# VectorE takes over the subtractions that split projected node rows, with four places for a group's rows

## The chip, the cores and the metric

The kernel runs on one core of a Trainium2 chip. The metric is the device time of one execution in microseconds (us); lower is better. Engines: TensorE (PE, and PEld for its weight loads), VectorE (DVE), ScalarE (ACT), GpSimd (POOL) and SyncE (SP), whose instructions here only issue DMAs.

## The reference

A graph attention layer and a mixture-of-experts layer, over 6250 nodes of 256 values and 100000 edges sorted by target:

```python
h = (layernorm(x) @ W.T).reshape(n, H, D)                 # H = 8 heads, D = 32
enc = relu(edge_attr @ edge_W.T + edge_b).reshape(-1, H, D)
alpha = einsum(h[src], a_src) + einsum(h[dst], a_dst) + sum(enc * h[dst], -1)
alpha = where(alpha >= 0, alpha, 0.2 * alpha)
ex = exp(alpha - segment_max(alpha, dst)[dst])
attn = ex / maximum(segment_sum(ex, dst)[dst], 1e-10)
x = x + (segment_sum(h[src] * attn[..., None], dst).reshape(n, H * D) + bias)
# then: x = x + top-2-of-8 experts (layernorm(x)), each gelu(xe @ W1 + b1) @ W2 + b2
```

The change is in the part that makes `h` and the tables of it.

## The kernel before

The program is five stages, one after the other, each its own block with a barrier of all engines at its end: `prepare`, `edges`, `attend`, `route`, `experts`. The order of the instructions of each engine is written out by hand; an engine waits on semaphores.

`prepare` is the first stage. The 49 tiles of 128 nodes come in `GROUPS` = 7 groups of `GT` = 7. For a tile TensorE turns x (`turn`, L413), ScalarE copies the turned tile out of PSUM (`take_xT`, L336), TensorE multiplies it by the weights (`project`, L429), and ScalarE scales the product into the group's place in SBUF (`take_h`, L347). VectorE makes the statistics of a group ahead of that (`statistics` L511, `merge` L130 to L137) and the reciprocal of its deviations (`deviations`, L519), for which ScalarE makes the root (`deviation`, L331).

A group's finished rows go two ways. SP stores them in DRAM in the table `h_tab`, from which the second stage gathers (`tables`, L276). And each float32 row is split into three bf16 parts that stay in SBUF: first = bf16(h), rest = h - first, second = bf16(rest), third = rest - second. For groups 0 to 5 GpSimd does all four (L241, L243, L245, L247), one group after the other through one buffer `rest`. Group 6 is split by VectorE in the second stage (`part`, L1094 to L1100). The rows of a group lie in one of three places, `c.stage[i % 3]`; `take_h` of a group's first tile waits until the group three before it has been stored and its `rest` made.

Beside this VectorE and ScalarE split the edges' attributes of four blocks in the same way: `first_part` and `second_part` are roundings on ScalarE (L365, L369), put in its list of tiles at tiles 25, 30, 35, 40 and five tiles later; `without_first` and `third_part` are subtractions on VectorE (L555, L560), at the end of its list behind `targets` (L538, L540), `same_node` (L544 to L549) and `split_weights` (L470 to L478). SP stores each block (`attributes`, L281), in one list with the tables of the groups: attributes 0, table 3, attributes 1, table 4, and so on. TensorE turns the list of targets behind group `REL_AT` (`turn_list`, L437), ScalarE copies it in the group behind that (`turn_back`, L357).

`edges` begins behind the barrier: SP loads the lists of targets (L730) and the attributes (L740), GpSimd waits for all tables and gathers rows of `h_tab` (L717), TensorE starts with L882 and L898, VectorE with L985, L993; the first messages are L1003.

Of the kernel before, what the change touches and what calls it, by code (L numbers as in the profile page):

```python
# [94 lines left out]
REST_WORDS = GT * IN  # L95
ROWS_AT = ACC_AT - RING * U * TW
# [19 lines left out]
def parts_of(c, i):  # L116

    h = c.stage[i % 3].rearrange("p (k h f) -> p k h f", h=H, f=FW)[:, :, :, 1:D + 1]
    rest = c.arena[:, LISTS:LISTS + REST_WORDS].rearrange("p (k h f) -> p k h f", k=GT, h=H)
    group = c.arena[:, PARTS_AT + i * GT * ST:PARTS_AT + (i + 1) * GT * ST].bitcast(BF16).rearrange("p (k q h f) -> p k q h f", k=GT, q=PARTS, h=H)  # L120
    return (h, rest, *(group[:, :, q] for q in range(PARTS)))
# [18 lines left out]
def prepare(nc, c, d):  # L140

    with ExitStack() as ctx:
# [3 lines left out]
         turned_back, derived, links_made, ends_same, cut, rests, cast) = semaphores(  # L146
# [3 lines left out]
            "p_turned", "p_back", "p_derived", "p_links", "p_endsame", "p_cut", "p_rests", "p_cast")  # L150
# [42 lines left out]
        pieces = [lists.take(PW).bitcast(BF16).rearrange("p (j f k e) -> p j f k e", j=PARTS, f=EF, k=U) for g in range(SG)]  # L193
        rel, link = lists.take(SG * UE).rearrange("p (g e) -> p g e", g=SG), lists.take(SG * UE)
# [17 lines left out]
        REL_AT = 3  # L212
# [6 lines left out]
        def _(pool):  # L219
# [18 lines left out]
            for i in range(GROUPS - 1):  # L238
                h, rest, first, second, third = parts_of(c, i)
                pool.wait_ge(h_copied, (i + 1) * GT + 2)  # L240
                nc.gpsimd.tensor_copy(first, h).then_inc(cast, 1)  # L241
                pool.wait_ge(cast, 4 * i + 1)
                nc.gpsimd.tensor_tensor(rest, h, first, ALU.subtract).then_inc(cast, 1)  # L243
                pool.wait_ge(cast, 4 * i + 2)
                nc.gpsimd.tensor_copy(second, rest).then_inc(cast, 1)  # L245
                pool.wait_ge(cast, 4 * i + 3)
                nc.gpsimd.tensor_tensor(third, rest, second, ALU.subtract).then_inc(cast, 1)  # L247
                pool.wait_ge(cast, 4 * i + 4)

        @block.sync  # L250
        def _(sp):
# [6 lines left out]
            sp.wait_ge(zeros_made, 5)  # L258
# [14 lines left out]
            def tables(n):  # L273
                i, k0, k1 = cuts[n]
                sp.wait_ge(h_copied, i * GT + k1 + 2)
                sp.dma_start(d.h_tab[(i * GT + k0) * P:(i * GT + k1) * P, :].rearrange("(k p) n -> p k n", p=P),  # L276
                             c.stage[i % 3][:, k0 * TW:k1 * TW].rearrange("p (k n) -> p k n", k=k1 - k0)).then_inc(rows_stored[i], 16)
# [32 lines left out]
        def _(act):  # L310
# [27 lines left out]
            def take_h(i, k):  # L338
                act.wait_ge(h_made, i * GT + (k + 3))
                if k == 0:  # L340
                    act.wait_ge(rs_made, i + 1)
                    if i >= 3:
                        act.wait_ge(rows_stored[i - 3], 32)
                        act.wait_ge(cast, 4 * (i - 3) + 2)
                n = i * GT + k
                to = c.stage[i % 3][:, k * TW:(k + 1) * TW].rearrange("p (h f) -> p h f", f=FW)[:, :, 1:FW]
# [13 lines left out]
            def first_part(g):  # L360
# [3 lines left out]
                act.wait_ge(stats, 2 * GT)  # L364
                nc.scalar.copy(pieces[g][:, 0], values[g]).then_inc(cut, 1)  # L365
# [87 lines left out]
        def _(dve):  # L453
# [30 lines left out]
            nc.vector.memset(c.stage[0].rearrange("p (n f) -> p n f", f=FW)[:, :, 0], 1.0).then_inc(zeros_made, 1)  # L484
            nc.vector.memset(two_stages.rearrange("p (n f) -> p n f", f=FW)[:, :, 0], 1.0).then_inc(zeros_made, 1)
# [75 lines left out]

            for k in range(GT):
# [44 lines left out]
            group(4)  # L607
            deviations(3)
            group(5)
            group(6)  # L610
            for i in range(4, GROUPS):
# [4 lines left out]
            for g in range(SG):  # L616
                without_first(g)
                third_part(g)
# [1280 lines left out]
```

## Time and profile before

| | us |
|---|---|
| median of 3 runs (2117.72 to 2121.09) | 2120.4 |
| time of the profiled execution | 2123.07 |
| its span | 2121.2 |
| PE, DVE, ACT, POOL busy | 1928.2, 1542.0, 1260.7, 1248.5 |
| first stage: last GpSimd instruction ends, first DMA of the second stage | 115.38, 116.54 |

All times below are from the span's start. A row of the timeline gives start, duration, engine, line, operation, output<-input, shapes, the number of instructions merged, and in brackets how long the engine was idle before and what ended that. A duration holds the time in which an instruction, once started, could not go on.

### The profile page before, as it was taken

Reading aid. Unit: us, or ns where it says so; the run is one execution under the profiler, and the core shown is the slowest. Engines: PE = TensorE matmul, PEld = TensorE weight load, DVE = VectorE, ACT = ScalarE, POOL = GpSimd, SP = SyncE. Lnnn points to the kernel's source line nnn. Section 1 sums busy time; section 2 is a strip of 40 time slices with the busy share of each in tenths; the row PEclk is TensorE's granted clock in tenths of the full one; section 3 lists DMA queues with packets and bytes.
Section 4 is the critical chain, followed back from the end, with each engine's and each line's share of the span. In section 5 each row is a group of like instructions: output and inputs, shape, how many; then the busy total and the mean of one; then the engine's idle time right before and its main releaser. Section 6 shows DMA issues by size and latency. Waiting matters only on the chain. (4 is left out here: it accounts for less than half of the span.)

```text
span 2121.2 us, 45176 instructions
## 1 busy us (share of the span) xinstructions
PE 1928.2 (91%) x12492; PEld 1499.8 (71%) x12492; DVE 1542.0 (73%) x3518; ACT 1260.7 (59%) x3557; POOL 1248.5 (59%) x1149
## 2 busy tenths in 40 slices
PE   7559899999999999999999666899999999999997
PEld 5426566666666666666666334899999999999996
DVE  7749899999999999999999887544444444444442
ACT  3438788888888888888888565433333333333332
POOL 5777777777777776666665000355555555555553
PEclk9769999999999999999999877999999999999998
DMA  9355555555555555555444596122222222222221
GB/s 250 108 155 156 153 151 156 156 153 154 152 158 149 148 150 142 150 143 143 141 136 120 208 346 130 48 36 36 41 36 36 40 37 36 38 38 36 38 39 23
DMA packets 161229, 242.11 MB, mean 114 GB/s; under 512 B 36895, under 2 KB 115519, under 8 KB 160866
## 3 DMA queue, kind: packets, MB, share of 16 engines
q0 software_dynamic: 61920, 139.45, 27.6%
q1 hardware_dynamic: 90362, 92.12, 14.7%
q10 hardware_dynamic: 8712, 7.65, 1.1%
q8 instruction: 117, 1.92, 0.4%
q14 instruction: 118, 0.97, 0.2%
HBM read 202.22 MB, written 36.91 MB: 113 GB/s over the span
## 5 line engine op out<-in xcount | busy, mean ns | idle before, releaser
L717 POOL DMA_INDIRECT arena<-h_tab,src x784 | 752.9, 960 | 291.1 <-issue 201.7
L1737 ACT ACTIVATE arena<-psum,arena 128x128 f32<-128x128 f32 x840 | 239.5, 368 | 519.0 <-PE psum L1687 519.0
L919 PE MATMUL psum<-arena 128*128 128x264 f32 x1760 | 475.1, 393 | 1.4 <-DVE arena L1016 1.4
L1687 PEld LDWEIGHTS psum<-arena 128*128 128x128 f32 x3360 | 393.1, 193 | 7.7 <-issue 2.4
L1687 PE MATMUL psum<-arena 128*128 128x128 f32 x3360 | 393.7, 276 | 2.0 <-DVE arena L1759 2.0
L898 PE MATMUL psum<-arena 128*128 128x256 bf16 x2640 | 376.3, 278 | 17.6 <-DVE arena L993 17.5
L1703 PE MATMUL psum<-arena 128*128 x1680 | 379.8, 379 | 0.0
L1649 POOL DMA_INDIRECT out_rows<-arena,src x105 | 212.5, 2024 | 250.4 <-DVE arena L1772 247.5
L919 PEld LDWEIGHTS psum<-arena 128*128 128x128 f32 x1760 | 299.6, 190 | 83.7 <-issue 47.9
L898 PEld LDWEIGHTS psum<-arena 128*128 x2640 | 246.1, 98 | 133.2 <-issue 69.6
L1703 PEld LDWEIGHTS psum<-arena 128*128 128x128 f32 x1680 | 311.1, 190 | 38.0
L790 ACT ACTIVATE arena<-iota_row,nrel 128x128 f32<-128x128 f32 x880 | 301.8, 392 | 55.3 <-PE psum L919 54.1
L993 DVE SCALAR_TENSOR_TENSOR arena<-arena,a_dst,psum 128x512 f32<-128x512 f32 x440 | 324.4, 737 | 11.5 <-ACT arena L783 7.4
L1003 DVE TENSOR_TENSOR arena<-arena,psum 128x528 f32<-128x528 f32 x440 | 305.1, 693 | 0.0
L1769 DVE TENSOR_TENSOR arena<-psum,arena 128x256 f32<-128x256 f32 x105 | 44.6, 425 | 290.6 <-PE psum L1703 290.6
L783 ACT ACTIVATE arena<-psum 128x1024 f32<-128x1024 f32 x220 | 221.7, 1008 | 23.9 <-PE psum L882 23.9
L1016 DVE TENSOR_TENSOR arena<-arena,psum 128x264 f32 x440 | 185.4, 421 | 28.3 <-PE psum L919 20.8
L794 ACT ACTIVATE arena<-arena,ones 128x512 f32<-128x512 f32 x220 | 158.8, 722 | 7.1
L1759 DVE TENSOR_SCALAR arena<-psum,ln_g,ln_b 128x128 f32<-128x128 f32 x210 | 76.5, 406 | 110.1 <-PE psum L1675 110.1
L1749 DVE COPY arena<-arena 128x1024 f32 x210 | 136.0, 690 | 18.4 <-PE psum L1687 3.9
L1635 POOL DMA_INDIRECT arena<-xn,src x103 | 101.6, 987 | 74.1 <-PE psum L1675 73.8
L801 ACT ACTIVATE arena<-ones 128x528 f32 x220 | 138.9, 631 | 0.0
(241 smaller groups left out, 1965.2 us busy)
## 6 DMA issues: line engine op xcount, KB each, us to landing
arena<-rel_list SPq DMA_DIRECT2D x110, 256.0 KB
arena<-h_tab,src POOLq DMA_INDIRECT x784
arena<-ea_slots SPq DMA_DIRECT2D x440, 27.0 KB
arena<-in_x SPq DMA_DIRECT2D x12, 896.0 KB, 12.8
arena<-in_W SPq DMA_DIRECT2D x16, 512.0 KB, 8.2
arena<-in_W SPq DMA_DIRECT2D x8, 1024.0 KB, 12.2
h_tab<-arena SPq DMA_DIRECT2D x6, 952.0 KB, 7.9
out_rows<-arena SPq DMA_DIRECT2D x5, 896.0 KB, 12.0
```

The lines of the kernel that those rows point to most:

```text
L717: pool.indirect_dma_start(rows[:, (p % RING * U + k) * TW:(p % RING * U + k + 1) * TW], None, d.h_tab[:, :], bass.IndirectOffsetOnAxis(ap= ...
L783: nc.scalar.activation(renc[:, g % RENC, :, :], ps[:, ENC:ENC + 2, :], ACT.Relu).then_inc(relu_done, 1)
L790: nc.scalar.activation(oh[:, a % OH, k, :], c.iota_row[:, :], ACT.Square, bias=c.nrel[:, a * U + k:a * U + k + 1]).then_inc(square_made, 1)
L898: last = nc.tensor.matmul(ps[:, HDT + x, y * UE:(y + 1) * UE], parts[:, ds(j * (PARTS * IN) + (q * IN + x * P), P)], oht[:, half % OT, (u ...
L919: last = nc.tensor.matmul(ps[:, AGG + a % 2, 0:HS], oh[:, a % OH, k, :], msg[:, a % MSG, k, :], start=(k == 0), stop=(k == U - 1))
L993: nc.vector.scalar_tensor_tensor(part, part, c.a_dst[:, x:x + 1], ps[:, HDT + x, :], ALU.add, ALU.mult).then_inc(prod_made, 1)
L1003: nc.vector.tensor_tensor(msg[:, a % MSG, :, :].rearrange("p k (h f) -> p k h f", h=H), row, weights.unsqueeze(3).to_broadcast([P, U, H, D ...
L1016: nc.vector.tensor_tensor(a_j, a_j, ps[:, AGG + a % 2, 0:HS], ALU.add).then_inc(acc_made, 1)
L1649: pool.indirect_dma_start(d.out[:, :], bass.IndirectOffsetOnAxis(ap=c.lists[:, n, 0:1], axis=0), y[:, n % 2, :], None, compute_op=ALU.add) ...
L1687: last = nc.tensor.matmul(ps[:, UP + 2 * b + h // 4, h % 4 * P:(h % 4 + 1) * P], w_now[:, b, m, h * P:(h + 1) * P], xT[:, b, m * P:(m + 1) ...
L1703: last = nc.tensor.matmul(ps[:, DOWN + b, 0:IN], hT[:, b, h * P:(h + 1) * P], w2[:, ds(e_now * (HC * IN) + h * IN, IN)], start=(h == 0), s ...
L1737: last = nc.scalar.activation(hT[:, b, h * P:(h + 1) * P], ps[:, UP + 2 * b + half, h % 4 * P:(h % 4 + 1) * P], ACT.Gelu, bias=b1_now[:, b ...
```

## The change

In the first stage the two subtractions of each group's split move from GpSimd to VectorE: `without_first_part` (rest) and `last_part` (third part), each 128x1792 elements, six of each. GpSimd keeps the two roundings of each group, and the second one waits for VectorE's subtraction (semaphore `left`). VectorE's list gets the twelve instructions at the places shown below. A group's rows lie in one of four places by the table `STAGE_OF`; the fourth place lies on the memory of attribute blocks 2 and 3, so ScalarE's `first_part(2)` waits until the rows of group 3 are stored and their `rest` is made. `take_h` waits for the group four before it, from group 4 on. `turn_list` moves from behind group 3 to behind group 4, and with it `turn_back`. VectorE clears one more column of ones at the start.

GpSimd's list, at the first two groups; before:

```order
L241 CAST arena<-arena 128x7x256 [waits p_hcopied]
L243 TENSOR_TENSOR arena<-arena 128x1792 [waits p_cast]
L245 CAST arena<-arena 128x7x256 [waits p_cast]
L247 TENSOR_TENSOR arena<-arena 128x7x256 [waits p_cast]
L241 CAST arena<-arena 128x7x256 [waits p_hcopied,p_cast]
```

and now (L244 and L246 are the roundings that were L241 and L245):

```order
L239 DMA arena<-in_ea_rows,arena 128x1024 x4
L244 CAST arena<-arena 128x7x256 [waits p_hcopied]
L246 CAST arena<-arena 128x7x256 [waits p_left]
L244 CAST arena<-arena 128x7x256 [waits p_hcopied]
L246 CAST arena<-arena 128x7x256 [waits p_left]
```

The two subtractions are gone, and the second rounding waits for VectorE.

The end of VectorE's list in the first stage, from the last instruction of `split_weights` on; before:

```order
L478 CAST ew<-arena 128x256 [waits p_derived]
L555 TENSOR_TENSOR arena<-arena 128x768 [waits p_cut]
L560 TENSOR_TENSOR arena<-arena 128x768 [waits p_rests,p_cut]
L555 TENSOR_TENSOR arena<-arena 128x768 [waits p_cut]
L560 TENSOR_TENSOR arena<-arena 128x768 [waits p_rests,p_cut]
L555 TENSOR_TENSOR arena<-arena 128x768 [waits p_rests,p_cut]
```

and now (L557 and L562 are the attributes' subtractions, L569 is `without_first_part`, L575 `last_part`):

```order
L479 CAST ew<-arena 128x256 [waits p_derived]
L557 TENSOR_TENSOR arena<-arena 128x768 [waits p_cut]
L569 TENSOR_TENSOR arena<-arena 128x1792 [waits p_left,p_cast]
L562 TENSOR_TENSOR arena<-arena 128x768 [waits p_rests,p_cut]
L575 TENSOR_TENSOR arena<-arena 128x7x256 [waits p_left,p_cast]
L569 TENSOR_TENSOR arena<-arena 128x1792 [waits p_left,p_cast]
L557 TENSOR_TENSOR arena<-arena 128x768 [waits p_cut]
L575 TENSOR_TENSOR arena<-arena 128x7x256 [waits p_left,p_cast]
L562 TENSOR_TENSOR arena<-arena 128x768 [waits p_rests,p_cut]
```

Eight subtractions of 1792 elements (groups 2 to 5) stand between the eight of 768. The other four stand earlier, between the statistics of groups 4 and 6.

ScalarE's list, at the first tile of group 3; before:

```order
L336 COPY arena<-psum 128x256 [waits p_h,p_xT]
L347 ACTIVATE arena<-psum,arena 128x8x33 [waits group0,p_cast,p_rs,p_h]
```

and now:

```order
L334 COPY arena<-psum 128x256 [waits p_h,p_xT]
L345 ACTIVATE arena<-psum,arena 128x8x33 [waits p_rs,p_h]
```

The wait for the store of group 0 (`group0`) has gone from there to the first tile of group 4.

```diff
+STAGE_OF = (1, 2, 0, 3, 1, 2, 0)
...
-    h = c.stage[i % 3].rearrange("p (k h f) -> p k h f", h=H, f=FW)[:, :, :, 1:D + 1]
+    h = c.stage[STAGE_OF[i]].rearrange("p (k h f) -> p k h f", h=H, f=FW)[:, :, :, 1:D + 1]
...
+        late_pieces = c.arena[:, lists.at - 2 * PW:lists.at]
+        c.stage.append(late_pieces[:, 0:GT * TW])
...
-        REL_AT = 3
+        REL_AT = 4
...
                 pool.wait_ge(h_copied, (i + 1) * GT + 2)
                 nc.gpsimd.tensor_copy(first, h).then_inc(cast, 1)
-                pool.wait_ge(cast, 4 * i + 1)
-                nc.gpsimd.tensor_tensor(rest, h, first, ALU.subtract).then_inc(cast, 1)
-                pool.wait_ge(cast, 4 * i + 2)
+                pool.wait_ge(left, 2 * i + 1)
                 nc.gpsimd.tensor_copy(second, rest).then_inc(cast, 1)
-                pool.wait_ge(cast, 4 * i + 3)
-                nc.gpsimd.tensor_tensor(third, rest, second, ALU.subtract).then_inc(cast, 1)
-                pool.wait_ge(cast, 4 * i + 4)
...
-                    if i >= 3:
-                        act.wait_ge(rows_stored[i - 3], 32)
-                        act.wait_ge(cast, 4 * (i - 3) + 2)
+                    if i >= 4:
+                        act.wait_ge(rows_stored[i - 4], 32)
+                        act.wait_ge(left, 2 * (i - 4) + 1)
...
                 act.wait_ge(stats, 2 * GT)
+                if g == 2:
+                    act.wait_ge(rows_stored[3], 32)
+                    act.wait_ge(left, 7)
                 nc.scalar.copy(pieces[g][:, 0], values[g]).then_inc(cut, 1)
...
+            def without_first_part(i):
+                h, rest, first, _, _ = parts_of(c, i)
+                dve.wait_ge(cast, 2 * i + 1)
+                if i:
+                    dve.wait_ge(left, 2 * i)
+                nc.vector.tensor_tensor(rest, h, first, ALU.subtract).then_inc(left, 1)
+
+            def last_part(i):
+                _, rest, _, second, third = parts_of(c, i)
+                dve.wait_ge(cast, 2 * i + 2)
+                dve.wait_ge(left, 2 * i + 1)
+                nc.vector.tensor_tensor(third, rest, second, ALU.subtract).then_inc(left, 1)
...
             group(4)
+            without_first_part(0)
+            last_part(0)
+            without_first_part(1)
             deviations(3)
             group(5)
             group(6)
+            last_part(1)
...
-            for g in range(SG):
-                without_first(g)
-                third_part(g)
+            without_first(0)
+            without_first_part(2)
+            third_part(0)
+            last_part(2)
+            without_first_part(3)
+            without_first(1)
+            last_part(3)
+            third_part(1)
...
+            without_first_part(5)
+            third_part(3)
+            last_part(5)
+            dve.wait_ge(left, 2 * (GROUPS - 1))
```

## Rows read from the trace of the kernel before

**Rows 1.** The page, TensorE's busy tenths in 40 slices of 53 us.

```profile
PE   7559899999999999999999666899999999999997
```

**Rows 2.** Windows, the longest gap (us, busy us of each engine, PEclk, DMA share, GB/s).

```profile
63.00:81.00 18.00, 0.76 (x5) 0.41 (x3) 17.86 (x12) 0.00 (x0) 16.17 (x6) 0.65 0.06 15
```

**Rows 3.** Waits of the first stage: us in total, times, longest us.

```profile
PE psum L429 <- ACT arena L336: 29.1, 7, 19.2
ACT arena L369 <- DVE arena L555: 18.1, 1, 18.1
ACT arena L347 <- DMA h_tab<-arena: 7.3, 1, 7.3
```

**Rows 4.** Timeline of POOL at the end of the first stage.

```profile
110.05 1.68 POOL L245 CAST arena<-arena 128x1792 bf16<-128x1792 f32 x1
111.81 3.57 POOL L247 TENSOR_TENSOR arena<-arena 128x1792 bf16<-128x1792 f32 x1
117.47 0.99 POOL L717 DMA_INDIRECT arena<-h_tab,src  x1 [2.09 <-issue]
```

**Rows 5.** Timeline of DVE ahead of the attributes' subtractions.

```profile
56.18 2.06 DVE L538 TENSOR_TENSOR arena<-arena 128x1024 f32<-128x1024 int32 x1
58.27 3.90 DVE L540 CAST arena<-arena 128x1024 bf16<-128x1024 f32 x1
76.07 3.75 DVE L476 SCALAR_TENSOR_TENSOR arena<-arena 128x256 f32<-128x256 bf16 x1
```

**Rows 6.** Timeline of POOL beside rows 5.

```profile
57.24 4.38 POOL L243 TENSOR_TENSOR arena<-arena 128x1792 f32<-128x1792 f32 x1
75.97 3.57 POOL L247 TENSOR_TENSOR arena<-arena 128x1792 bf16<-128x1792 f32 x1
```

**Rows 7.** DVE up to 140 us: groups with mean ns, and two single rows.

```profile
L1096 DVE TENSOR_TENSOR arena<-arena 128x1792 f32<-128x1792 f32 x1 | 2.0, 2015 | 0.0
L1100 DVE TENSOR_TENSOR arena<-arena 128x1792 bf16<-128x1792 f32 x1 | 2.0, 2012 | 0.0
...
14.09 0.42 DVE L529 SCALAR_TENSOR_TENSOR arena<-psum,arena 128x256 f32<-128x256 f32 x1 [2.22 <-PE psum L420]
82.79 0.95 DVE L555 TENSOR_TENSOR arena<-arena 128x768 f32<-128x768 f32 x1
93.39 4.27 DVE L555 TENSOR_TENSOR arena<-arena 128x768 f32<-128x768 f32 x1
```

**Rows 8.** Groups of POOL in the first stage: busy us, mean ns.

```profile
L243 POOL TENSOR_TENSOR arena<-arena 128x1792 f32<-128x1792 f32 x6 | 23.1, 3848 | 0.5
```

**Rows 9.** Timeline of DVE, a group's statistics and group 4's last merge.

```profile
27.60 2.38 DVE L511 BATCH_NORM_STATS2 arena<-arena 128x6 f32<-128x256 f32 x7
35.73 0.17 DVE L137 SCALAR_TENSOR_TENSOR arena<-arena 128x7 f32<-128x7 f32 x1
```

**Rows 10.** Timeline of ACT: two tiles in a row, and the last tile.

```profile
40.80 0.48 ACT L347 ACTIVATE arena<-psum,arena 128x264 f32<-128x264 f32 x1 [0.37 <-PE psum L429]
41.91 0.48 ACT L347 ACTIVATE arena<-psum,arena 128x264 f32<-128x264 f32 x1 [0.37 <-PE psum L429]
...
108.83 0.48 ACT L347 ACTIVATE arena<-psum,arena 128x264 f32<-128x264 f32 x1 [0.41 <-PE psum L429]
```

**Rows 11.** The line of the tables' stores (L276), its DMAs.

```profile
DMA to landing us min/median/max: 3.6/5.9/12.8
```

**Rows 12.** Timeline of PE: a tile's four matmuls without a gap, and behind two gaps.

```profile
40.82 1.06 PE L429 MATMUL psum<-arena 128*128 128x264 f32 x4
...
50.71 2.13 PE L429 MATMUL psum<-arena 128*128 128x264 f32 x4 [6.40 <-ACT arena L336]
123.70 0.61 PE L882 MATMUL psum<-arena,ew 30*128 30x512 bf16 x2 [14.90 <-DMA arena<-ea_slots]
```

**Rows 13.** Timeline of DVE, the first message, and windows of L717 on POOL.

```profile
161.13 0.69 DVE L1003 TENSOR_TENSOR arena<-arena,psum 128x528 f32<-128x528 f32 x1
...
150.00:200.00 50.00, 38.12 (x40) 0.90 0.53 152
```

## What the change should do to the time

> **What bounds the kernel now.** TensorE's busy tenths, read first, are 9 nearly everywhere; the hole at the left edge is the first stage, two slices of 53 us [rows 1]. The windows then show what the hole is: from 63 to 81 us TensorE and ScalarE do nothing, while VectorE and GpSimd are busy for 17.86 and 16.17 of 18 us [rows 2]. The waits say who holds whom: TensorE waits 29.1 us for ScalarE's copies, and ScalarE 18.1 us for VectorE's first attribute subtraction (L555) and 7.3 us for the store of group 0 [rows 3]. The timeline of GpSimd says what ends the stage: its last subtraction ends at 111.81 + 3.57 = 115.38, and the second stage's first DMA follows at 116.54, so the barrier costs 1.16 [rows 4]. ScalarE's last tile is done at 109.31 [rows 10]. So GpSimd's list ends last, and behind the barrier everything moves with it.
>
> Why VectorE is slow there: L476 works on 256 elements and takes 3.75 us [rows 5]; an instruction of that kind and size took 0.42 with GpSimd idle [rows 7]. It ends at 79.82, GpSimd's subtraction beside it at 75.97 + 3.57 = 79.54 [rows 6]. It goes both ways: GpSimd's L243 of 57.24 takes 4.38 behind VectorE's L538, which ends at 58.24 [rows 5, 6]. The two engines take turns, a whole instruction each, wherever VectorE has such operands; its statistics are not held (2.38 for seven) [rows 9]. The Trainium skill, page "SBUF — State Buffer", section "Who interferes with whom", says the same for VectorE instructions with two SBUF inputs against a GpSimd instruction that reads SBUF: whichever starts first holds the port pair, the other "fully blocks". By that rule the new subtractions and the roundings add up; without it the rival "no turns" below would hold. The trace agrees with it (3.75 against 0.42).
>
> **The change, part by part.**
> Removed: twelve GpSimd subtractions, 3.85 us each by the mean of L243 (23.1 for six) [rows 8], 46 us in all. L476, L540 and the first L555 no longer wait behind them.
> Added on VectorE: twelve of 1792 elements. Group 6's same two, done by VectorE in the second stage, took 2.015 and 2.012 [rows 7]: 24 us in all, of which eight (16.1) lie in the list's tail. GpSimd keeps 12 roundings of 1.68 [rows 4].
>
> The walk of VectorE's list, 0.05 us for each hand-over. Its merge of group 4 ends at 35.9 [rows 9], and GpSimd's first rounding is then done. Then they alternate: subtraction, rounding, subtraction, rounding of group 1, subtraction: 3 x 2.0 + 2 x 1.7 = 9.4, to 45.3. Two groups of statistics and merges, 2 x (2.4 + 0.6) = 6.0, and one wait of a merge behind a rounding, about 1.0: 52.3. The last subtraction of group 1: 54.3. Now GpSimd stands still (it waits for group 2's rest), so `targets`, `same_node` and `split_weights` go at their own speed. I price them by elements: 2.01 / 1792 is 1.1 ns for one; four instructions of about 1020 are at most 4.5, five of 256 at no more than 0.42 [rows 7] are 2.1, three reciprocals and the small ones 0.6: 7.2 at most. The own part of L538, from the end of the rounding it waited for, is 1.07, so I take 6.0, and 5.5 and 7.2 as ends. That makes 60.3; before, L476 alone ended at 79.82 [rows 5].
>
> The tail: 8 x 2.01 = 16.1, and 8 attribute subtractions of 0.95 [rows 7] = 7.6. Of GpSimd's roundings, seven fall in it (second of groups 2 to 5, first of 3 to 5), and in this order each stands between two of VectorE's instructions, whether by a semaphore or by the turns: 7 x 1.68 = 11.8. Sum 35.5, hand-overs 0.5: VectorE ends at 96.3, the barrier at 97.5 instead of 116.54: **19.0 less**.
>
> What lies beside it. ScalarE no longer waits at group 3 for the store, but for the deviations that VectorE makes only at 45.4; it is ready at about 42.7 (tile at 41.91, its 0.48 [rows 10], a copy): 7.3 become 2.7. From there 28 tiles at 1.11 (41.91 - 40.80 [rows 10]) are 31.1, eight roundings of attributes and the small ones 7.6, waits for VectorE's merge of group 6 (3) and for the three rests of attributes (2, 4 and 2): some 94 to 95, less overlaps, so 93 to 94. Then SP issues the last store (0.7). TensorE turns one list later, hidden in its waits. ScalarE's list has 1 to 2 us of slack. The store of group 3 now sits behind attributes 0 and is issued at 64.5; ScalarE's `first_part(2)` wants it at 73. With the median landing of 5.9 it is there; with the longest, 12.8, it comes at 77.3 and ScalarE is 4 us late [rows 11]. The memset (0.1 us) hides in VectorE's wait for x.
>
> The second stage begins with loads behind the last store, which lands at least 3.6 after its issue [rows 11], thus at 98 to 100 where it used to be there before the barrier. I bound that at 0 to 1.3 us and take 0.5. GpSimd's gathers must wait for it too, up to 1.5 us more; they are hidden: the first message is at 161.13, 44 us behind the first gather at 117.47 [rows 4, 13], and by then 35 gathers at 50 / 40 = 1.25 us are issued [rows 13] where two are needed.
>
> Sum: 19.0 - 0.5 = 18.5. Against the profiled execution's 2123.07 that is 2104.6; that execution lies 2.7 above the median of the runs, 2120.4, so the same sum from the median gives **2101.9**.
>
> **The rivals.**
> *ScalarE and TensorE end last.* TensorE has gaps of 4 to 6 us at the waits for rests; behind one of 6.40 a tile's four matmuls took 2.13 instead of 1.06 [rows 12], and over the long gap the granted clock was 0.65 [rows 2]. Two such gaps cost about 2 us each, and a late store of group 3 up to 4. ScalarE then ends at 97 to 100, the barrier is at 98.5 to 101: 15.5 to 18 less, 2103 to 2106. Against it: VectorE's sum barely notices, so this costs only what passes the slack.
> *No turns for these.* Subtractions and roundings overlap. Then VectorE's list is no bound; ScalarE's tiles with few waits end near 86, the barrier is at 88: 28 less, 2092. Against it: rows 5 to 7.
> *Every subtraction is held as long as L555 was*, 4.27 instead of 0.95 [rows 7]: if VectorE's 2.01 became 4.3 beside GpSimd and the DMAs of this stage, twelve times 2.3 is 27.6, the stage ends at 125 and the kernel is **slower**, 2120.4 + 8.6 = 2129. It decides from 3.6 us for one subtraction on (12 x 1.6 = 19). Against it: the 4.27 is 0.95 and the rest of a GpSimd subtraction, and those are gone; only roundings of 1.68 are left, which the sum holds already.
> *The gain doesn't arrive.* The stage ends early, but the second stage starts no earlier, or is held by the gathers: 2120. For it: GpSimd issues gathers without a pause at the start (38.12 of 50 us busy, the rest issue [rows 13]). Against it: the 44 us lead.
>
> **How the numbers follow.** Forecast 0.74; ScalarE last 0.15; no turns 0.04; held subtractions 0.03; gain doesn't arrive 0.04. A measurement of this kernel can tell about 0.2%, 4.2 us, from no change. Faster: the first three, 0.93; same 0.04; slower 0.03. The range: the forecast's own is 2099 to 2106 (walk of the lists between +1.2 and -0.5, roundings of 1.68 to 1.85, DMA start 0 to 1.3, 1.7 for the runs' spread). TensorE is at a low clock at the start of the second stage (behind the gap of 14.90 [rows 12]); the gap shrinks, and how long the clock stays low could shift 3 us either way. That gives 2096 to 2109, with the second case in it.
>
> **What would show it.** VectorE's L569 and L575 at 2.0 us, up to 3.7 when a rounding is ahead; GpSimd's roundings the only instructions of its list; the rest of attributes 0 made at 61 instead of 81; ScalarE with no gap over 5 us; VectorE's last L575 ends at 96, the second stage's first DMA at 97.5; from there on everything as before, 19 us earlier. Wrong if L569 takes over 3 us with no rounding beside it, if ScalarE's last tile comes behind VectorE's end by over 2 us, or if the first message is not 19 us earlier.

## The result, and the profile after

| | before | after |
|---|---|---|
| median of 6 runs, us | 2119.9 (2117.0 to 2128.64) | 2105.66 (2101.48 to 2107.36) |
| profiled execution: time, span | 2123.07, 2121.2 | 2104.89, 2103.0 |
| second stage: first DMA | 116.54 | 95.52 |
| first gather | 117.47 | 99.50 |
| first message, last message | 161.13, 1194.2 | 143.04, 1176.4 |

The changed kernel is faster: 0.9927 of the time before, with the interval 0.9907 to 0.9947, or 11 to 20 us. The medians differ by 14.2 us, the two profiled executions by 18.2. The forecast was 2101.9 us in a range of 2096 to 2109: the time lies in the range, 3.8 above the number.

More line numbers have moved than the ones named above: L276 is L274, L347 is L345, L365 is L366, L369 is L370, L717 is L750, L783 is L816, L835 is L868 and L1003 is L1036. The experiments' kernels have a line or a few more or less, so each is read by its operation and shape.

The page after, the span, GpSimd's and TensorE's busy time and their tenths:

```profile
span 2103.0 us, 45182 instructions
...
PE 1926.2 (92%) x12492; PEld 1499.6 (71%) x12492; DVE 1539.6 (73%) x3531; ACT 1261.2 (60%) x3557; POOL 1206.3 (57%) x1137
...
PE   7679999999999999999999486899999999999997
...
POOL 3377777777777776666664000455555555555553
```

TensorE's hole at the left edge is now a 6 and a 7, where both were 5 [rows 1]; its fifth slice is a 9 where it was an 8, and the slices at the end of the second stage come 18 us earlier; the rest of the row is as it was. GpSimd is busy for 42 us less, VectorE for 2 us less although it took over twelve instructions: a duration holds the time in which an instruction stands behind the other engine's, so what VectorE got in work it lost in waiting.

VectorE's list after, the timeline of three pieces:

```profile
39.81 3.47 DVE L575 TENSOR_TENSOR arena<-arena 128x1792 bf16<-128x1792 f32 x1 [1.78 <-POOL arena L246]
43.38 2.02 DVE L569 TENSOR_TENSOR arena<-arena 128x1792 f32<-128x1792 f32 x1
...
52.17 2.02 DVE L575 TENSOR_TENSOR arena<-arena 128x1792 bf16<-128x1792 f32 x1
...
54.35 1.18 DVE L540 TENSOR_TENSOR arena<-arena 128x1024 f32<-128x1024 int32 x1
...
59.30 0.49 DVE L477 SCALAR_TENSOR_TENSOR arena<-arena 128x256 f32<-128x256 bf16 x1
...
60.03 0.95 DVE L557 TENSOR_TENSOR arena<-arena 128x768 f32<-128x768 f32 x1
60.90 2.02 DVE L569 TENSOR_TENSOR arena<-arena 128x1792 f32<-128x1792 f32 x1
62.84 0.95 DVE L562 TENSOR_TENSOR arena<-arena 128x768 bf16<-128x768 f32 x1
65.36 3.47 DVE L575 TENSOR_TENSOR arena<-arena 128x1792 bf16<-128x1792 f32 x1 [1.57 <-POOL arena L246]
68.93 2.03 DVE L569 TENSOR_TENSOR arena<-arena 128x1792 f32<-128x1792 f32 x1
...
89.61 2.42 DVE L562 TENSOR_TENSOR arena<-arena 128x768 bf16<-128x768 f32 x1
91.95 2.01 DVE L575 TENSOR_TENSOR arena<-arena 128x1792 bf16<-128x1792 f32 x1
94.99 0.06 DVE L1110 MEMSET arena<- 128x2 f32 x1 [1.03 <-PEq L143]
```

The instruction of `split_weights` that took 3.75 takes 0.49 [rows 5]. A subtraction of 1792 takes 2.02, or 3.47 where a rounding stands ahead of it; one of 768 takes 0.95 or 2.42. VectorE's last one ends at 91.95 + 2.01 = 93.96. Its first instruction of the second stage, the memset, comes at 94.99.

GpSimd's roundings beside these, from its timeline:

```profile
62.98 2.34 POOL L246 CAST arena<-arena 128x1792 bf16<-128x1792 f32 x1 [14.21 <-DVE arena L569]
65.28 1.68 POOL L244 CAST arena<-arena 128x1792 bf16<-128x1792 f32 x1
...
99.50 0.97 POOL L750 DMA_INDIRECT arena<-h_tab,src  x1 [8.28 <-DMA h_tab<-arena]
```

The second rounding of group 2 is ready when the subtraction ahead of it ends at 62.92, and stands behind VectorE's L562 (2.34 us, against 1.68 without that); the next, at 65.28, is the one behind which L575 stands from 65.36 on. GpSimd has waited for VectorE for 14.21 us before. Its last rounding of the stage ends at 91.22, ahead of VectorE's last instruction, so its list no longer ends the stage. It waits 8.28 us for the last store before it can gather.

ScalarE after, at the places the forecast named, its last tile, and a copy of gathered rows:

```profile
45.61 0.48 ACT L345 ACTIVATE arena<-psum,arena 128x264 f32<-128x264 f32 x1 [2.65 <-DVE arena L521]
...
61.02 0.83 ACT L370 CAST arena<-arena 128x768 bf16<-128x768 f32 x1 [0.70 <-DVE arena L557]
...
71.86 0.83 ACT L370 CAST arena<-arena 128x768 bf16<-128x768 f32 x1 [3.94 <-DVE arena L557]
73.08 0.83 ACT L366 CAST arena<-arena 128x768 bf16<-128x768 f32 x1 [0.40 <-DMA h_tab<-arena]
...
93.10 0.48 ACT L345 ACTIVATE arena<-psum,arena 128x264 f32<-128x264 f32 x1 [0.41 <-PE psum L430]
...
116.29 0.22 ACT L868 COPY arena<-arena 128x16 f32 x1 [3.98 <-POOLq L738]
```

SyncE's queue after, the last store and the first load of the second stage:

```profile
92.46 1.96 SPq L274 DMA_DIRECT2D h_tab<-arena  x2
95.52 0.33 SPq L763 DMA_DIRECT2D arena<-rel_list  x1
```

The wait of 18.1 us for the first attribute subtraction is 0.70 (at 61.02); the longest wait for such a subtraction is now the one for the second block, 3.94. At group 3, where the wait for the store of group 0 was 7.3, it is 2.65, and for another thing, the deviations [rows 3]. The last tile is done at 93.58, where it was 109.31 [rows 10]. SyncE issues the second piece of the last store behind it, until 94.42: 0.46 later than VectorE's last instruction ends. The memset of 94.99 follows 0.57 behind that. So in this execution it is not VectorE's list, nor GpSimd's, but the last store's issue that opens the barrier, by half a microsecond. That is less than what repeats of this first stage show: in a1, below, which has the same first stage, VectorE ends at 94.83 and SyncE's last issue at 94.63.

Behind the barrier 3 of the 21 us are lost again: the first DMA is 21.0 earlier, the first gather 18.0, the first message 18.1. ScalarE's waits for gathered rows (the releaser is POOLq, GpSimd's sequencer, which passes on that rows have landed) and for projected attributes, 95 to 175 us, first of before and then of after:

```profile
ACT arena L783 <- PE psum L882: 23.9, 5, 15.0
...
ACT arena L835 <- POOLq L705: 2.3, 2, 2.2
```

```profile
ACT arena L868 <- POOLq L738: 14.2, 7, 4.0
ACT arena L816 <- PE psum L915: 14.1, 5, 9.4
```

ScalarE, whose list feeds the first messages, waits longer for rows that GpSimd has gathered, 14.2 us against 2.3. That is not because this window holds more of the second stage: from each kernel's barrier to its first message the same two sums are 14.2 and 2.3.

### The profile page after: what moved, and what is told of

Same layout as the page of the kernel before. It is cut to its first block and busy times, and to the rows that moved or that the text cites. A ratio compares the mean times of both kernels' runs of the same rounds, so it can differ in the third digit from the quotient of the medians.

```text
span 2103.0 us, 45182 instructions
## 1 busy us (share of the span) xinstructions
PE 1926.2 (92%) x12492; PEld 1499.6 (71%) x12492; DVE 1539.6 (73%) x3531; ACT 1261.2 (60%) x3557; POOL 1206.3 (57%) x1137
## 5 line engine op out<-in xcount | busy, mean ns | idle before, releaser
L750 POOL DMA_INDIRECT arena<-h_tab,src x784 | 757.6, 966 | 294.0 <-issue 191.2
L931 PE MATMUL psum<-arena 128*128 128x256 bf16 x2640 | 376.3, 278 | 19.1 <-DVE arena L1026 18.9
L1026 DVE SCALAR_TENSOR_TENSOR arena<-arena,a_dst,psum 128x512 f32<-128x512 f32 x440 | 325.2, 739 | 10.7 <-ACT arena L816 7.1
L1036 DVE TENSOR_TENSOR arena<-arena,psum 128x528 f32<-128x528 f32 x440 | 306.0, 695 | 0.6 <-PE psum L982 0.6
L816 ACT ACTIVATE arena<-psum 128x1024 f32<-128x1024 f32 x220 | 221.7, 1008 | 14.1 <-PE psum L915 14.1
```

The lines of the kernel that those rows point to most:

```text
L750: pool.indirect_dma_start(rows[:, (p % RING * U + k) * TW:(p % RING * U + k + 1) * TW], None, d.h_tab[:, :], bass.IndirectOffsetOnAxis(ap= ...
L816: nc.scalar.activation(renc[:, g % RENC, :, :], ps[:, ENC:ENC + 2, :], ACT.Relu).then_inc(relu_done, 1)
L931: last = nc.tensor.matmul(ps[:, HDT + x, y * UE:(y + 1) * UE], parts[:, ds(j * (PARTS * IN) + (q * IN + x * P), P)], oht[:, half % OT, (u ...
L1026: nc.vector.scalar_tensor_tensor(part, part, c.a_dst[:, x:x + 1], ps[:, HDT + x, :], ALU.add, ALU.mult).then_inc(prod_made, 1)
L1036: nc.vector.tensor_tensor(msg[:, a % MSG, :, :].rearrange("p k (h f) -> p k h f", h=H), row, weights.unsqueeze(3).to_broadcast([P, U, H, D ...
```

## The experiments

Every kernel of this section carries one common edit in the second stage: a value of a list on which an engine waits is raised to at least 0, and GpSimd raises one more semaphore for each pair. b0 is the kernel before with that edit alone, a0 the changed one. b1 and a1 are the same two kernels once more.

```diff
-                    pool.wait_ge(msg_made, last[q % CS])
+                    pool.wait_ge(msg_made, smax(last[q % CS], 0))
+                    pool.sem_inc(passed, 1)
...
-                act.wait_ge(rows_in, t_next[u])
+                act.wait_ge(rows_in, smax(t_next[u], 0))
```

The eight runs b0 to e5 fell on two chips on which each kernel needs some 460 us more, the kernel before too (2582.1 and 2585.16). The four runs e1, e2, e7 and e6 fell on a third, where the kernel before takes 2121.88. There is no plain run of b0 or a0 on that one, so the common edit's own cost is not known there. On the first two chips the first stage is as elsewhere; in the second all engines have gaps together. TensorE's busy time while the messages are made, from the windows of b0 and of before:

```profile
600.00:1200.00 600.00, 458.02 (x2504) 291.70 (x2505) 397.63 (x926) 353.03 (x922) 291.45 (x306) 0.86 0.37 101
```

```profile
600.00:1176.00 576.00, 546.77 (x3511) 364.64 (x3512) 551.14 (x1303) 489.05 (x1307) 386.59 (x405) 1.00 0.50 141
```

Where 3 us of the second stage's start are asked for, such gaps blur the time, and from the barrier on they blur the trace too. Between the barrier and the first message VectorE stands for 16.3 to 36.7 us in waits that the profile puts down to no engine and no DMA of the core ("remote"). ScalarE, which waits for gathered rows for 14.2 us there in the changed kernel of the other chips, does not wait for them once in any of the eight. So until the barrier and the first gather these traces can be compared; whether a late gather delays the first message they cannot test.

### b0 and a0: the two kernels with the common edit

> The kernel before, with one edit in the second stage that every experiment has: GpSimd's and ScalarE's waits on a value of the slot lists are waits on max(value, 0), which adds a register instruction to each, and on GpSimd one semaphore increment per pair. It is the base for the others. Expected: GpSimd's distance from gather to gather is 0.05 to 0.15 us longer for a pair; the first stage as before (barrier at 116.5). Both theories: 2118 to 2140 us, by how far GpSimd's pace carries to the end.

> The changed kernel with the same edit of the waits. Both theories: 14 to 19 us below b0, barrier at 95.5, first gather at 99.5.

Measured: b0 2604.83 us, 1.0078 of before (1.0051 to 1.0104); a0 2580.07, 0.9988 (0.9966 to 1.0011). The common edit costs 22.7 us on this chip, and the change takes 24.8 off. The first stage is the known one: b0's first gather stands at 117.53, a0's at 99.27. That this is more than the 14 to 18 us of the plain kernels is not explained by anything in the first stage; comparisons down to e5 are with a0 and b0 or a1 and b1.

### e3: two microseconds more on VectorE's list

```diff
             last_part(5)
+            last_part(5)
+            dve.wait_ge(left, 2 * (GROUPS - 1) + 1)
```

> The changed kernel with last_part(5) done twice, the second time behind the first (same values), so VectorE's list is 2.0 to 2.1 us longer and nothing else. Theory G (the second stage's start is held by the gathers, which wait for the last rows' store to land at 99.5, 4 us behind the barrier): barrier at 97.5, first gather still at 99.5, time within 0.7 us of a0. Rival B (the barrier decides what follows): everything behind it 2 us later, time a0 + 2.

Measured: 2585.95 us, 1.0001 (0.9975 to 1.0027), 5.9 above a0, with intervals that overlap. VectorE's list, SyncE's queue and GpSimd's in e3:

```profile
92.46 4.08 DVE L576 TENSOR_TENSOR arena<-arena 128x1792 bf16<-128x1792 f32 x2 [1.57 <-POOL arena L247]
97.12 0.06 DVE L1114 MEMSET arena<- 128x2 f32 x1 [0.57 <-PEq L144]
```

```profile
91.32 2.51 SPq L275 DMA_DIRECT2D h_tab<-arena  x2
97.05 0.33 SPq L767 DMA_DIRECT2D arena<-rel_list  x1
```

```profile
97.98 0.97 POOL L754 DMA_INDIRECT arena<-h_tab,src  x1 [5.56 <-DMA h_tab<-arena]
```

Here VectorE ends last, at 96.54, and the memset comes 0.58 behind it, just as it comes 0.57 behind SyncE's last issue in the changed kernel. In a0 that memset is at 94.83: the barrier moves by 2.3. The first gather is at 97.98, 1.3 *earlier* than a0's 99.27, and the first message is at 175.57, 2.1 later than a0's 173.43. So the last store's landing is not the same moment in both kernels. That the first message moved with the barrier and not with the gather is what rival B says, but it can't be held against theory G: ScalarE waits for no gathered row here, in e3 or in a0, and b1 and e4b, with barriers 1.0 apart, have first messages 5.6 apart.

### e4: later gathers in the kernel before

```diff
+            for n in range(16):
+                if n:
+                    pool.wait_ge(passed, n)
+                pool.memset(c.place_i[:, :], 0).then_inc(passed, 1)
+            pool.wait_ge(passed, 16)
```

> The kernel before (b0) with 16 small memsets one after the other on GpSimd ahead of its first gather, so that the gathers start some 2.5 to 4 us later against the barrier (117.5 becomes 120 to 121.5), as they do in the changed kernel; TensorE and VectorE start as before. Theory G: ScalarE's copies of gathered rows (L835 of the kernel before) hold its list, and the first message (161.1) comes later by the same 2.5 to 4 us; time b0 + 2.5 to 4. The prediction's step (44 us of lead hide it): first message at 161, time b0 within 0.7.

Measured: 2596.73 us, 1.0051 (1.0028 to 1.0074). The first gather is at 121.07, 3.5 later than b0's; the first message is at 192.1, b0's at 193.1. A gather that starts 3.5 us later delays no message here, where nothing waits for the rows. The time is 8 us below b0's, for an edit that only adds work; so on these chips the second stage answers to an edit in ways of its own, and such a difference in time says nothing of the first stage.

### b1, a1 and e4b: the same three kernels once more

> The kernel of b0 again, in another job, as the base of this one: in the job of b0 all engines stood still together for up to 30 us at a time in the second stage, the kernel before as well (2582 us), which buries effects of 2 to 4 us. Both theories: 2120 to 2140 us if those pauses are gone, first message at 161.

> The kernel of a0 again. Both theories: 14 to 19 us below b1; first gather 99.3 to 99.5, first message 143.

> The kernel of e4 again: gathers of the kernel before begin at 121.1 instead of 117.5 (seen in e4). Theory G (gathers hold the second stage's start through ScalarE's copies of gathered rows): first message 3 to 4 us later than in b1, time b1 + 3 to 4. The prediction's step (hidden by 44 us of lead): first message as in b1, time within 0.7.

Measured: b1 2607.54 us, 1.0097 (1.0064 to 1.013); a1 2584.08, 0.9989 (0.9965 to 1.0014); e4b 2593.19, 1.0051 (1.0028 to 1.0073). The three ratios repeat to within 0.002. First gather and first message: b1 118.0 and 194.0, a1 98.4 and 173.1, e4b 120.4 and 188.4. Again a later gather makes no later message, and the message is 5.6 earlier, which is the size of what the gaps do to it. That the longer list is the faster one, by 14 us this time, repeats too, and stays unexplained.

### e5: the last stores in another order

SyncE issues the first piece of group 6's table ahead of attributes 3.

```diff
+            tables(6)
...
-            for n in range(6, len(cuts)):
-                tables(n)
+            tables(7)
```

> The changed kernel (a1) with SyncE's order changed at the end of the first stage: the table of group 6's first four tiles is stored ahead of attributes 3 instead of behind it. Theory G: that store goes out at 90.3 instead of 92.5, the last one at 93.6 instead of 94.1 with less ahead of it, so it lands at 97.5 to 98.5 instead of 99.3, the gathers and the first message come 1 to 2 us earlier, time a1 - 1 to 2. Rival B (the barrier at 95.5 decides, which doesn't move): first message and time as a1 within 0.5.

Measured: 2579.27 us, 0.9979 (0.9954 to 1.0004), a1 on the same chip 0.9989. The first gather comes at 97.67 instead of 98.43, the first message at 172.5 instead of 173.1. That is 0.8 and 0.6 us, between what the theory and the rival expected, and nothing that the time can show: 4.8 us less, with intervals that overlap.

### e1: the four places without the move

GpSimd makes all four parts again and VectorE's list is the old one; `STAGE_OF`, `REL_AT` and the waits of the fourth place stay. The cut is against the kernel before and leaves out the table and the memory of the fourth place, which are those of the changed kernel.

```diff
-                    if i >= 3:
-                        act.wait_ge(rows_stored[i - 3], 32)
-                        act.wait_ge(cast, 4 * (i - 3) + 2)
+                    if i >= 4:
+                        act.wait_ge(rows_stored[i - 4], 32)
+                        act.wait_ge(cast, 4 * (i - 4) + 2)
...
+                if g == 2:
+                    act.wait_ge(rows_stored[3], 32)
+                    act.wait_ge(cast, 14)
```

> The places alone: four places for a group's rows, turn_list behind group 4 and first_part(2)'s wait as in the changed kernel, but GpSimd makes all four steps of the split as before and VectorE's list is the old one. Theory T (the two engines' shared turns set the end): GpSimd still has 6 x 10.5 us of work and VectorE still waits behind its subtractions, so the barrier moves from 116.5 to 112 to 114; ratio to the kernel before 1.003 to 1.008 (b0 1.0078 and 1.0097, the edit of the waits, less 3 us). Rival P (the places carry the gain, since TensorE waited 29 us for ScalarE): barrier near 100, ratio near 1.000.

Measured: 2124.11 us, 1.0008 (0.9997 to 1.0018): no change, and below the 1.003 to 1.008 that was expected, which came from what the common edit cost on the other chips. GpSimd's last subtraction and SyncE's first load in e1:

```profile
110.20 3.57 POOL L251 TENSOR_TENSOR arena<-arena 128x1792 bf16<-128x1792 f32 x1
...
115.85 0.99 POOL L739 DMA_INDIRECT arena<-h_tab,src  x1 [2.08 <-DMA h_tab<-arena]
```

```profile
114.93 0.33 SPq L752 DMA_DIRECT2D arena<-rel_list  x1
```

The first stage ends 1.6 us earlier than before (113.77 instead of 115.38), and still with GpSimd's list. So of the wait of 7.3 us [rows 3] at most 1.6 had been on the path: ScalarE's wait for the first attribute subtraction grew from 18.1 to 19.7, and its last tile ends at 109.26 (109.31 before). The time doesn't show the 1.6, but this kernel carries the common edit and the kernel before doesn't.

### e2: the move without the fourth place

The cut is against the changed kernel; it leaves out the memory of the fourth place and its column of ones.

```diff
-STAGE_OF = (1, 2, 0, 3, 1, 2, 0)
+STAGE_OF = (0, 1, 2, 0, 1, 2, 0)
...
-        REL_AT = 4
+        REL_AT = 3
...
-                    if i >= 4:
-                        act.wait_ge(rows_stored[i - 4], 32)
-                        act.wait_ge(left, 2 * (i - 4) + 1)
+                    if i >= 3:
+                        act.wait_ge(rows_stored[i - 3], 32)
+                        act.wait_ge(left, 2 * (i - 3) + 1)
...
-                if g == 2:
-                    act.wait_ge(rows_stored[3], 32)
-                    act.wait_ge(left, 7)
```

> The move alone: VectorE makes the subtractions in the new order, but a group's rows lie in three places as before (turn_list behind group 3, take_h waits for the group three before it). Theory T: the wait for group 0's store (to 49 to 50 us) delays group 3 by 4 us, which ScalarE's later waits for VectorE swallow; VectorE's last subtraction at 94 to 96, barrier at 95.5 to 97.5, ratio within 0.002 of a0's 0.9988. Rival P: barrier at 103 or later.

Measured: 2105.26 us, 0.9923 (0.9909 to 0.9936), the whole gain of the change (0.9927), although this kernel carries the common edit. Against e1, which carries it too, it is 18.9 us. ScalarE, VectorE and SyncE in e2:

```profile
46.77 0.48 ACT L344 ACTIVATE arena<-psum,arena 128x264 f32<-128x264 f32 x1 [4.27 <-DMA h_tab<-arena]
...
91.92 0.48 ACT L344 ACTIVATE arena<-psum,arena 128x264 f32<-128x264 f32 x1 [0.41 <-PE psum L426]
```

```profile
91.56 2.03 DVE L570 TENSOR_TENSOR arena<-arena 128x1792 bf16<-128x1792 f32 x1 [1.58 <-POOL arena L245]
94.16 0.06 DVE L1106 MEMSET arena<- 128x2 f32 x1 [0.57 <-PEq L144]
```

```profile
94.09 0.33 SPq L759 DMA_DIRECT2D arena<-rel_list  x1
```

With three places ScalarE is 1.2 us late at group 3 (46.77 against 45.61), and yet its last tile ends at 92.40, 1.2 *earlier* than with four. In e2 no `first_part` waits for a store, and `turn_back`'s copies stand at 63 to 66 us, where ScalarE is about to wait 3.65 us for VectorE anyway; in the changed kernel they stand at 79 to 82, behind that wait. The five traces with the changed kernel's first stage (after, a0, a1, e3, e5) have that tile's end between 93.44 and 94.24, so 92.40 is outside what repeats show. Here VectorE ends last (93.59), as the forecast had it, and the memset is 0.57 behind. The second stage's first load is 1.4 us earlier than in the changed kernel, the first message 3.4 earlier (139.6). By the last message 0.6 of it is left (1175.8 against 1176.4), and the spans are 2102.9 and 2103.0.

### e7 and e6: an order of VectorE's list that might beat both

e7 puts the statistics of group 5, group 2's subtraction, the attributes' subtractions and the last parts of groups 3 and 4 at other places of VectorE's list; e6 is e7 with group 5's last part in the second stage and e5's order of stores.

```diff
-        DEVIATIONS = {(0, 0): (1,), (1, 0): (2,), (2, 3): (3,), (3, 3): (4, 5, 6)}
+        DEVIATIONS = {(0, 0): (1,), (1, 0): (2,), (2, 3): (3,), (3, 4): (4, 5, 6)}
...
             without_first_part(0)
+            group(5)
             last_part(0)
             without_first_part(1)
             deviations(3)
-            group(5)
             group(6)
             last_part(1)
+            without_first(0)
+            without_first_part(2)
...
-            without_first(0)
-            without_first_part(2)
             third_part(0)
             last_part(2)
+            without_first(1)
             without_first_part(3)
-            without_first(1)
+            third_part(1)
+            without_first(2)
             last_part(3)
-            third_part(1)
             without_first_part(4)
-            without_first(2)
-            last_part(4)
             third_part(2)
             without_first(3)
+            last_part(4)
             without_first_part(5)
```

> The changed kernel with another order of VectorE's list (statistics of group 5 between the subtractions of group 0, the rests of attributes 0 ahead of targets, those of 1 and 2 earlier, ScalarE's deviations 4 to 6 one tile later). Same instructions. Theory T: the sum of VectorE's and GpSimd's turns stays, less about 2 us of waits for roundings that now have other work in them; ScalarE's last tile at 89 to 91 instead of 93.6; VectorE's end at 92 instead of 94, barrier 93.5, last store landed by 96; ratio 0.001 to 0.002 below a0's 0.9988. If only one engine's own waits counted, nothing would move.

> e7, and the last subtraction of group 5 moved to the start of the second stage, where VectorE waits for the first list of targets, and SyncE's order of e5. Theory T: VectorE's list 2 us shorter, the barrier then goes by its attributes' last part and SyncE's last store: barrier 91.5 to 92.5, first gather at 94 to 95.5, first message some 4 us earlier than in a0; ratio 0.0015 to 0.003 below a0's. Rival: the loads of the second stage and the last store are in each other's way, and gathers start at 97 all the same.

Measured: e7 2108.01 us, 0.9934 (0.9921 to 0.9947); e6 2108.94, 0.9942 (0.9928 to 0.9955). Neither beats e2 or the changed kernel, and neither stage ended where it was expected: the memset behind the barrier is at 98.03 in e7 (93.5 expected) and at 95.88 in e6 (91.5 to 92.5). ScalarE at the place that went wrong in e7 and its last tile; VectorE behind it; and SyncE's stores from 60 us on, by their line:

```profile
75.49 0.83 ACT L367 CAST arena<-arena 128x768 bf16<-128x768 f32 x1 [6.62 <-DMA h_tab<-arena]
...
95.91 0.48 ACT L346 ACTIVATE arena<-psum,arena 128x264 f32<-128x264 f32 x1 [0.41 <-PE psum L431]
```

```profile
76.36 0.96 DVE L558 TENSOR_TENSOR arena<-arena 128x768 f32<-128x768 f32 x1 [5.55 <-ACT arena L367]
...
95.43 2.03 DVE L576 TENSOR_TENSOR arena<-arena 128x1792 bf16<-128x1792 f32 x1 [1.57 <-POOL arena L247]
```

```profile
L275 SPq DMA_DIRECT2D h_tab<-arena x5: 359/617/1967, 65.6 to 96.4; - x5
...
DMA to landing us min/median/max: 3.9/4.7/9.7
```

`first_part(2)` reaches its place at 68.9 and waits 6.62 us for group 3's store. That was issued at 65.63 and took the longest time to land, 9.7 us. This is the wait that the fourth place brings. It holds ScalarE, and then VectorE for 5.55 us, and the stage ends 2.4 us later than in the changed kernel (first load at 97.96). e6 has the same wait, 6.72 us behind a store that took 9.8. e7's trace is of the slowest of its six executions (2111.56, median 2108.01); e6's is of its fastest (2106.14). The order might have won what this wait took; on three places it was not tried, so that is not shown.

## Why the prediction was right

**The turns and the walk of VectorE's list: right.** The fifth instruction of the alternation ends at 45.40 (forecast 45.3), the last subtraction of group 1 at 54.19 (54.3), and the first attribute subtraction starts at 60.03 (60.3). The middle part, from there on, took 5.8 where I took 6.0 between 5.5 and 7.2. The rule of the Trainium skill, page "SBUF — State Buffer", section "Who interferes with whom", is borne out by 3.47 and 2.42 behind a rounding against 2.02 and 0.95 without one: one instruction waits until the other engine's is over, and doesn't run at half speed beside it. The rival "no turns" would have had the barrier at 88. No subtraction was held as long as the old L555: the longest is 3.47 with a rounding in it, under the 3.6 from which the slower case would have followed.

**The tail: right in kind, 2.1 us too long.** Forecast 60.3 to 96.3, measured 60.03 to 93.96. The seven roundings are all there, four as waits and three inside durations: 4 x 1.57 + 3 x 1.46 = 10.7, which is 1.52 for each where I took 1.68. The sixteen subtractions are then 33.9 - 10.7 = 23.2 instead of 23.7: one starts 1.94 or 0.87 behind the one ahead of it, not 2.02 and 0.95. The hand-overs of 0.5 are not to be seen. That is 1.1 + 0.5 + 0.5 = 2.1.

**ScalarE's list: right.** Its first wait was to shrink to 2.7 and is 2.65. The last tile was to end at 93 to 94 and ends at 93.58, though with luck in the terms: the waits for three rests were put at 2, 4 and 2, and are 0.70, 3.94 and none; waits of up to 1.58 for TensorE, which the sum had left out, fill most of the difference. Group 3's store was to be issued at 64.5 and wanted at 73; it was issued at 64.22, took 8.7 to land where I took the median of 5.9, and was waited for 0.40 us until 73.08. That a long landing makes ScalarE late, as the text said, did not happen here and happened in e7 and e6.

**What ends last: wrong by half a microsecond in this trace.** With VectorE's tail shorter, the list of ScalarE and the store behind it were no longer covered. The last issue ends at 94.42, VectorE at 93.96. It is the mechanism of the first rival, though with ScalarE done at 93.6 and not at 97 to 100. e3, e2 and a1 show the other side: with VectorE last the memset comes 0.58, 0.57 and 0.57 behind its end. In a1, with the changed kernel's own first stage, that is by 0.20, so which of the two ends last changes from one execution to the next. The barrier's price of 1.16 was read where GpSimd ended last. The second stage's first DMA comes 1.10 behind the last store's issue here, but 0.50, 0.51 and 0.50 behind VectorE's end in e2, e3 and a1: for a forecast in which VectorE ends last that term was 0.66 too high.

**The start of the second stage: the step that failed.** "They are hidden" was said of the gathers, by the 44 us between the first gather and the first message, and 0.5 us was set for this start. The barrier came 21.0 earlier instead of 19.0, the first message 18.1 instead of the 19 that "What would show it" asked for: 2.9 were given back. The last store was to land at 98 to 100, and the gathers, which wait for it, start at 99.50: 3.98 behind the second stage's first DMA, where it was 0.93. The lead of 44 us is no slack: ScalarE copies gathered rows in the same list that projects attributes and makes the blocks for the first messages, and waits up to 3.98 us for them. The experiments made for this, e3, e4 and e4b, don't settle whether the late gather is the cause, since in them nothing waits for gathered rows. The six traces of chips without gaps say more (us; the barrier by VectorE's memset behind it, the wait from there to the first message):

| | barrier | first gather | first message | ScalarE's waits for gathered rows |
|---|---|---|---|---|
| before | 116.61 | 117.47 | 161.13 | 2.3 |
| e1 | 115.00 | 115.85 | 159.97 | 2.2 |
| e2 | 94.16 | 97.18 | 139.60 | 11.6 |
| e6 | 95.88 | 98.73 | 141.81 | 10.2 |
| after | 94.99 | 99.50 | 143.04 | 14.2 |
| e7 | 98.03 | 101.11 | 143.74 | 12.6 |

The first message lies 42.4 to 44.1 behind the first gather, and 44.5 to 48.1 behind the barrier. In the four kernels with the move it comes in the order of the gathers, not of the barriers: e6 has its barrier 0.9 later than the changed kernel, its first gather 0.8 earlier, and its first message 1.2 earlier. That speaks for the gathers, which the forecast had called hidden; it is a comparison of kernels that differ in more than this, one trace each, and no edit moved the gather alone on such a chip.

e2 shows that it need not matter: its first message is 3.4 earlier than the changed kernel's, and the last message 0.6. What eats such a lead while the messages are made stays open.

The two errors, +2.0 at the barrier and -2.4 behind it, nearly cancel: the profiled executions differ by 18.2, forecast 18.5. The medians of the runs differ by 14.2; that is within the interval of 11 to 20, and the executions of the kernel before alone spread over 11.6 us. Against the profiled execution the forecast was 2104.6, and it took 2104.89; the 3.8 us by which the number is too low are no more than that spread, so they name no step. With either error alone the time would still lie in the range; that 18.2 is so close to 18.5 is owed to their opposite signs. This is luck in part only: an earlier barrier does not make the last store land earlier, and the gathers wait for that.

**The parts of the change.** The whole gain is the move (e2: 0.9923; against e1 18.9 us). The four places bring nothing that these times show, alone (e1: 1.0008) or on top of the move (0.9927 against 0.9923). Both comparisons set a kernel with the common edit beside one without it; by the traces the places are worth 1.6 us alone, and on top of the move the first load comes 1.4 later with them. The forecast shortened ScalarE's wait at group 3 from 7.3 to 2.7 and left open what of this was worth anything, since it named VectorE as last. With the move alone the wait is 4.27 (e2), and the 1.2 us that the fourth place saves there are lost again, and as much once more, by the time of the last tile. No run separates the two things that the move does, that GpSimd's list loses six subtractions of 3.85 us and six of at least 3.57, and that VectorE's short instructions no longer stand behind them; both are seen in the trace.

## What to carry to other kernels

When two engines take turns at SBUF, look at what work stands on both sides of the turn: the same split takes 2 us an instruction on one engine and 3.6 to 3.9 on the other, and the slower one also stretched a short instruction of its neighbour from 0.49 to 3.75. Before a buffer is added to end a wait, ask which list ends the stage, and whether the new buffer's own neighbours bring another wait: here that wait was 0.4 us in one order of the list and 6.6 in another. Before an experiment is made on another chip, look whether the wait that it is about is there at all. A long lead between a first transfer and the work that needs it is no proof of slack: name each engine between them whose list is kept in order, and what it waits for.

## What was not expected of the hardware

- A rounding of 1.68 us costs VectorE 1.46 to 1.57 when the two alternate, and VectorE's subtractions start up to 0.08 us before the one ahead of them is shown as ended.
- The stores of the table issued from 60 us on landed between 4.7 and 8.7 us after their issue in the changed kernel, and between 3.9 and 9.7 in e7. The last store, behind which GpSimd waits, let the first gather start at 99.27 with the next stage's loads coming at 95.34 (a0), and at 97.98 with those loads at 97.05 (e3). a1, the same kernel as a0, had it at 98.43, so 0.8 of the 1.3 us is within what repeats of one kernel show.
- On two chips the same program took 2582.1 and 2585.16 us instead of 2119.9, behind the first stage, the cause unknown, with TensorE at 458 of 600 us where it has 547 of 576. And there the common edit cost 22.7 us, while e1, which has it too, is 2.2 us above the kernel before on the chip without such gaps.
